# GpSimd multiplies the states with C two slots at a time: a ring of eight, and a weight tile moved to a shared place

## What is computed

```python
def step(h, inp):
    u_t, d_t, b_t, c_t = inp
    dA = jnp.exp(d_t[..., None] * A)
    h = dA * h + (d_t * u_t)[..., None] * b_t[:, :, None, :]
    y = jnp.einsum('bkdn,bkn->bkd', h, c_t)
    return (h, y)
```

## Time and profile before

| what | value |
|---|---|
| median of 3 runs | 13330.74 us (13321.66 to 13340.04) |
| profiled execution, span | 13331.9 us |
| DVE busy | 11940.3 us, 90% |
| PE busy | 10547.0 us, 79% |
| POOL busy | 10383.8 us, 78% |
| ACT busy | 6832.0 us, 51% |
| transfers | 2404 MB, 61.1% of the 16 engines' time |

### The profile page before, as it was taken

The page is one execution under the profiler, slowest core; times in us unless marked ns, Lnnn a source line. Parts: engine busy times, 40 slices in busy tenths (PEclk is TensorE's granted clock), DMA queues, the critical chain, the costliest instruction groups (busy, mean ns, idle before and its releaser), DMA issues. The chain is left out here.

```text
span 13331.9 us, 95099 instructions
## 1 busy us (share of the span) xinstructions
PE 10547.0 (79%) x24646; PEld 4127.2 (31%) x24646; DVE 11940.3 (90%) x8647; ACT 6832.0 (51%) x10172; POOL 10383.8 (78%) x4597
## 2 busy tenths in 40 slices
PE   6777878778787787777878778777787777878778
PEld 2333323333233332333323333233332333323233
DVE  7999779997799978999789997799978999789997
ACT  4545555455555555555555555555555545555455
POOL 4999559994599945999459994599946999469994
PEclk8999988999889998999989999899998999988999
DMA  4676546764467644676446774467644677457774
GB/s 139 214 219 214 126 129 216 218 216 121 133 215 219 215 118 140 213 221 214 111 145 216 219 216 106 148 215 221 214 102 152 215 220 214 100 154 214 220 212 100
DMA packets 734798, 2404.29 MB, mean 180 GB/s; under 512 B 173200, under 2 KB 175248, under 8 KB 722768
## 3 DMA queue, kind: packets, MB, share of 16 engines
q1 hardware_dynamic: 734192, 2397.58, 61.1%
HBM read 2300.18 MB, written 67.11 MB: 178 GB/s over the span
## 5 line engine op out<-in xcount | busy, mean ns | idle before, releaser
L1261 POOL TENSOR_TENSOR state<-state,c_sb 128x1024 f32<-128x1024 f32 x3072 | 7182.5, 2358 | 464.2 <-ACT carry L1088 462.5
L1017 PE MATMUL ps<-state,wt 128*128 128x512 f32 x12288 | 6346.7, 659 | 164.0 <-ACT ya L1081 109.2
L1017 PEld LDWEIGHTS ps<-state,wt 128*128 128x128 f32 x12288 | 2558.9, 212 | 3061.6 <-issue 2490.5
L1220 DVE TENSOR_TENSOR_SCAN state<-decay,carry,ps 128x1024 f32<-128x1024 f32 x1440 | 3379.4, 2347 | 105.0 <-DVE ps L1207 38.9
L1088 ACT COPY carry<-state 128x1 f32<-128x1 f32 x3072 | 585.3, 191 | 4861.2 <-DVE state L1220 4852.1
L994 PE MATMUL ps<-parts,sel 114*128 114x512 bf16 (+1 forms) x3840 | 1288.7, 421 | 2083.4 <-DVE state L1220 2081.7
L1250 POOL TENSOR_TENSOR dbu<-b_sb,du 128x1024 f32<-128x1024 f32 x1152 | 2717.4, 2359 | 229.6 <-DVE du L1235 229.6
L1207 DVE TENSOR_TENSOR ps<-ps,du 128x1024 f32<-128x1024 f32 x1920 | 2323.4, 1210 | 0.9
L1130 ACT ACTIVATE decay<-delta,a_neg 128x1024 f32<-128x1024 f32 x1920 | 2194.9, 1144 | 6.9
L1220 DVE TENSOR_TENSOR_SCAN state<-ps,carry,dbu 128x1024 f32<-128x1024 f32 x864 | 2013.4, 2330 | 3.9 <-POOL dbu L1250 3.1
L994 PEld LDWEIGHTS ps<-parts,sel 114*128 114x128 bf16 (+1 forms) x3840 | 261.0, 100 | 3634.6 <-DVE state L1220 3361.7
(11 more groups left out here) (217 smaller groups left out, 10126.7 us busy)
## 6 DMA issues: line engine op xcount, KB each, us to landing
c_sb<-bc SPq DMA_DIRECT2D x2048, 512.0 KB, 4.3
c_sb<-bc SPq DMA_DIRECT2D x2048, 256.0 KB, 5.5
b_sb<-bc SPq DMA_DIRECT2D x768, 512.0 KB, 4.7
b_sb<-bc SPq DMA_DIRECT2D x768, 256.0 KB, 5.4
x_nat<-x SPq DMA_DIRECT2D x17, 1536.0 KB, 14.4
gates<-gate_a SPq DMA_DIRECT2D x8, 2048.0 KB, 6.8
x_tok<-x SPq DMA_DIRECT2D x288, 48.0 KB, 1.8
gn<-gn_t SPq DMA_DIRECT2D x8, 1536.0 KB, 7.3
```

The source lines that it names most:

```text
L1017: mm = pe.matmul(py[:, q * CH:(q + 1) * CH], col("ident"), state[:, slot(g, n), q * CH:(q + 1) * CH], start=(n == 0), stop=False)
L1220: dve.tensor_tensor_scan(state[:, slot(g, n), way], rate, what, 0.0 if fresh else carry[:, n:n + 1], ALU.mult, ALU.add)\
L1261: pool.tensor_tensor(state[:, slot(g, n), :], state[:, slot(g, n), :], c_sb[:, n % CRING, :], ALU.mult).then_inc(S["weighted"], 1)
```

## The change

`RING` becomes 8, so that neighbouring states always lie in neighbouring slots and a pair never wraps. POOL multiplies states n - 1 and n in one instruction of 128 x 2048 after every odd n (`times_c`), and one count of `weighted` now stands for a pair: PE and SP wait for pairs (`pair_of`). The product with B for state 2 of a chunk moves in front of the last pair of the chunk before, the one for the first chunk in front of everything. `B_AHEAD` is 5, which moves the B rows one state forward in SP's program. The eighth slot takes 4 KB per partition; to make room, `w_xp` lies in a place that the scan overwrites, is copied to DRAM once in the setup and loaded again for each image at the start of `prep_a`.

```diff
-RING = 7
+RING = 8
+PAIR = 2
-B_AHEAD = 4
+B_AHEAD = 5
...
+    xp_dram = nc.dram_tensor("xp", (128, 5 * 128), F32, kind="Internal").ap()
...
-    w_xp = put("w_xp", [128, 5, 128], F32)
...
+    w_xp = at("w_xp", [128, 5, 128], F32, C0 + 512 + 25088)
...
                 sp.wait_ge(S["w_loaded"], 80 + 16 * GROUPS)
+                sp.wait_ge(S["setup_dve"], 7)
+                sp.dma_start(xp_dram, w_xp[:, :, :].rearrange("p i c -> p (i c)")).then_inc(S["w_loaded"], 16)
+                sp.wait_ge(S["w_loaded"], 96 + 16 * GROUPS)
...
+                    sp.dma_start(w_xp[:, :, :].rearrange("p i c -> p (i c)"), xp_dram).then_inc(S["w_in_loaded"], 16)
                     sp.wait_ge(S["gn_ready"], NCH)
...
                         if j == 0:
-                            pe.wait_ge(S["w_in_loaded"], 64)
+                            pe.wait_ge(S["w_in_loaded"], 80)
...
+            def pair_of(g, n):
+
+                return (g * NS + n) // PAIR
...
-                            sp.wait_ge(S["weighted"], g * NS + n - CRING + 1 + CREDIT)
+                            sp.wait_ge(S["weighted"], pair_of(g, n) - CRING // PAIR + 1 + CREDIT)
...
-                        pe.wait_ge(S["weighted"], g * NS + n + 1 + CREDIT)
+                        pe.wait_ge(S["weighted"], pair_of(g, n) + 1 + CREDIT)
...
-                            if n + 2 in POOLED:
+                            if n > 0 and n + 2 in POOLED:
                                 times_b(T, c, POOLED.index(n + 2))
-                            pool.wait_ge(S["carried"], g * NS + n + 1 + CREDIT)
-                            pool.wait_ge(S[f"c_in_{n % CRING}"], c_landed(T, c, n))
-                            pool.tensor_tensor(state[:, slot(g, n), :], state[:, slot(g, n), :], c_sb[:, n % CRING, :],
-                                               ALU.mult).then_inc(S["weighted"], 1)
-
+                            if n == NS - 1 and following:
+                                times_b(*following, 0)
+                            if n % PAIR == PAIR - 1:
+                                times_c(T, c, n - PAIR + 1)
+
+                    def times_c(T, c, n):
+
+                        g = c + T * NSC
+                        pool.wait_ge(S["carried"], g * NS + n + PAIR + CREDIT)
+                        for m in range(n, n + PAIR):
+                            pool.wait_ge(S[f"c_in_{m % CRING}"], c_landed(T, c, m))
+                        both = state[:, slot(g, n):slot(g, n) + PAIR, :]
+                        pool.tensor_tensor(both, both, c_sb[:, n % CRING:n % CRING + PAIR, :], ALU.mult)\
+                            .then_inc(S["weighted"], 1)
+
+                    times_b(0, 0, 0)
                     each_chunk(steps)
```

More of the change, by code:

```diff
@@ L433, in _ @@
                                                          (DT0 + RANK * g, 2 * g + order, 6 * NS, RANK)):
-                                nc.vector.tensor_copy(w_xp[lo_p:hi_p, i, to:to + count],
-                                                      from_[lo_p:hi_p, st, src, first:first + count])
+                                last = nc.vector.tensor_copy(w_xp[lo_p:hi_p, i, to:to + count],
+                                                             from_[lo_p:hi_p, st, src, first:first + count])
+                last.then_inc(S["setup_dve"], 1)
             @block.tensor
```

## The result

The changed kernel takes 13515.22 us (median of 4 runs, 13500.7 to 13526.56) against 13333.18 us of the kernel before, run in turn with it: a ratio of 1.0139 [1.0127, 1.0151], slower by 182 us. That is 98 us above the forecast and 15 us above its range. The direction and the mechanism were forecast; the size was not.

A forecast was written before the change was run, and what follows sets the result against it. DVE was taken to set the pace, with POOL following with little room. Profiled 13331.9 us + 69 (bunched C loads) + 13 (image ends) + 4 (`w_xp` copy) = 13417.9, as a median of runs 13416.7; range 13335 to 13500.

The forecast's parts named there:

- Rival (A): Passes 2 and 5: queued half rows drain as fast as whole rows, bunches are absorbed; 13348 us, chance 0.28.
- rival (B): DVE's 109 us of standing still before L1220: POOL's shorter work removes four tenths; 13288 us, chance 0.05.
- rival (D): POOL's pairs wait for more than their own rows, so passes 0, 1, 3 and 4 wait too; no chance given.
- Rival (C): Passes 2 and 5 both stretch from their second chunk: pair 4.62 us or three rows 10 us; 13519 us, chance 0.12.
- The end of an image: Behind the last scan: last pair starts when carried, two rows added after; 1.6 us per image, 13 us for eight.
- Loads of C in bunches: Passes 2 and 5: C rows go out in twos or threes and land late; 8.6 us per image, 69 us in all.
- The other four passes: Passes 0, 1, 3 and 4: whole rows take some 1.5 us, three at most 7.1; no loss.
- Step "w_xp": Setup and `prep_a`: copying the weights out costs 4 us once; loading them back per image is hidden and costs nothing.

## Why the prediction was wrong in size and right in kind

**Right.** The price of the pair (4526 against 4527 ns). The Trainium skill (GPSIMD Engine Reference, section 3.1) gives 4497 ns for an addition of this size; the rows of the product have 4527 as the mean, 4495 at the least. That POOL's shorter work is worth nothing: the run with pairs from the third chunk shows 1.0001. That the three rows of a bunch take 9.5 us against 6.8 left, and two 7.2 (9.5 and 7.0 in the chunk shown): pass 2 lost 57.4 us where 56 were worked out (though not in the chunks where they were), with waits of 2.8, 0.2 and 2.5 us where 2.7, 0.4 and 2.7 were, and taking the third row away took the loss away. That passes 1, 3 and 4 lose nothing. Rival (A), absorbed bunches, is refuted by the halves everywhere; rival (B), a faster DVE, by the result, and by single products and pairs from chunk 2, at the time of before; rival (D) by passes 1, 3 and 4. Rival (C) named 13519, within 4 us of the result, by luck: neither did the pair cost 4.62 us nor three rows 10 us. The Trainium skill's fit for another issuing path (DMA: Bandwidth & Descriptors, part on the anatomy of one DMA), by which three rows would take an estimated 5.6 us, does not hold for these halves: with 5.6 us nothing would wait, and the traces have the waits.

**Step "The end of an image", and pass 5 in "Loads of C in bunches".** The working took 54.1 us as DVE's need in all four chunks of pass 5. That is its need in the second and third, and there the failed term is POOL's room: 4.8 us per image were to cover three chunks, and 14.7 us were lost in them, 1.8 per image. The last chunk needs 45.7 from scan 0 to scan 15. The budget that the working should have made: pair 0/1 starts 6.1 us after scan 0; six pairs and five B products must be done by the start of scan 15; 6.1 + 6 x 4.50 + 5 x 2.31 = 44.7 against 45.7. One us of room for 5.8 us of waits gives 4.8 us per image, and 5.35 were measured: 43 us, 30 more than the whole pass was given. Part of it needs no late row: without sums scan 10 is due at 30.0 and B10 is done at 31.0 by the working, and the run with whole rows keeps 3.8 us here. This is the largest part of the 98. The numbers for it stood in the working; the row on the last chunk's length (the trace of before has it) was not read.

The same mistake sized the end. The term 1.6 us supposed that the last pair starts when its second state is carried. It starts 2.5 us after the scan, since POOL is behind its own pair 12/13 and a row is late: 4.4 us per image, 35.1 in sum instead of 13. The late row is the smaller part, for whole rows keep 26.3 us of it. By the working's own prices pair 12/13 ends at 6.1 + 7 x 4.50 + 5 x 2.31 = 49.2, 1.1 us after the last scan would end. A term that says "starts when carried" is only right if POOL has caught up by then, and the working itself had POOL late in this pass.

**Step "The other four passes ... Nothing".** 21.6 us in pass 0, 14.7 in its first chunk and 6.3 in its second, because SP's program has sixteen other transfers between the first rows of C. The working looked for what a bunch carries among the rows of B, and not among these. Moving them behind gave back 16.9 us.

**Step "w_xp": 4 us.** 0.1 at the first scan. **Outside the scan: nothing was forecast, 17.6 us measured**, of which some 14 go with the granted clock of the stages outside. The forecast's sum had no term for that; its cause stays open.

By size, against the 86 us of the sum: pass 5 44.5 more, the end of the image 22.1, the first chunks 21.6, outside and setup 13.7, pass 2 and the rest 1.1. That is 103 us, the miss against the profiled execution.

## What to carry to other kernels

When a counter is made coarser (one count for two products), the loads behind it come in bunches, and a bunch holds whatever else stands between them in the issuing engine's program: list it, and put all that has no deadline behind the rows that have one. Work out room against deadline for each kind of chunk, the first and the last one above all, for there DVE has less to do and the same wait is dearer. And an engine that nobody waits for pays nothing for being made faster: here the pairs were worth nothing that could be told even in the passes in which they cost nothing.

## What the runs showed of the hardware that was not expected

- Loading a 512 KB row as two halves of 64 partitions costs nothing that can be told as long as rows are asked for one by one: 1.0007 [0.9997, 1.0017] with halves in all passes, at 88% to 93% busy transfer engines. With pairs the kernel with these transfers is 3.5% over the kernel before, and at 85% busy. So here the busy share said nothing of the time.
- The place of four rows of B per chunk, with equal bytes, is worth 105 us (1.0058 against 1.0139).
- GpSimd's product grows by 1084 ns per 512 columns over the three sizes seen: 1274 ns for 512, 2358 for 1,024, 4527 for 2,048.
- Stages that no edit touches differ by up to 9 us of 380 between images of kernels that are equally fast (376.7 against 385.7), in step with the granted clock (0.92 and 0.88). The seven stretches of before sum to 2684.9 us and those of single products to 2661.2, so differences of some 20 us between single executions can come from there.
